# A decoder block's early weight loads, zero fill and convolution taps in another order

## The reference

```python
x = x + attention0(layernorm(x))                    # Fourier features of q and kv, running sum over positions
x = x + conv0(layernorm(x), k, skip, ctx, ctx)      # the sublayer around the change
x = x + experts0(layernorm(x))                      # 8 experts, the best 2 for each row
x = x + attention1(layernorm(x))
x = x + cross_attention1(layernorm(x), ctx)
x = x + ternary_ffn1(layernorm(x))

def conv0(v, k, bias, x1, x2):                      # num_heads = 8, 16 groups, L = 256 channels
    vr, x1r, x2r = (t.reshape(B, 16, 8, L) for t in (v, x1, x2))
    kv = vr[:, :, :, None, :] * x2r[:, :, None, :, :]
    y = causal_convolution(kv, k)                   # by FFT in the reference: y[l] = sum over m <= l of k[l-m] kv[m]
    y = y + kv * skip
    return einsum('bhijl,bhil->bhjl', y, x1r)
```

## Time and profile before

| | |
|---|---|
| median of 3 executions | 808.7 us (807.49, 808.7, 815.94) |
| the profiled execution | 810.86 us |
| its span, first to last instruction | 809.0 us |
| PE, PEld busy | 626.0 us (77%), 440.7 us (54%) |
| DVE busy | 456.6 us (56%) |
| ACT busy | 321.5 us (40%) |
| POOL busy | 261.6 us (32%) |
| DMA | 50.01 MB, 62 GB/s over the span |
| mean granted clock of TensorE | 0.879 |

### The profile page before, as it was taken

The page is one execution under the profiler, slowest core; times in us unless marked ns, Lnnn a source line. Parts: engine busy times, 40 slices in busy tenths (PEclk is TensorE's granted clock), DMA queues, the critical chain, the costliest instruction groups (busy, mean ns, idle before and its releaser), DMA issues.

```text
span 809.0 us, 13184 instructions
## 1 busy us (share of the span) xinstructions
PE 626.0 (77%) x4335; PEld 440.7 (54%) x4338; DVE 456.6 (56%) x988; ACT 321.5 (40%) x754; POOL 261.6 (32%) x300
## 2 busy tenths in 40 slices
PE   3849897450599999997387998999988767774564
PEld 3446444430488988896363456555576346553233
DVE  4684999575355554553225153352547755777685
ACT  2503200424133343342233364553736445555353
POOL 5470588748000000000702882763904220000000
PEclk9969999555799999999558999999999988996697
DMA  9930001456611111111800000000000400000000
GB/s 328 375 123 1 0 0 60 148 164 239 198 50 33 49 52 52 52 40 37 244 8 0 1 1 0 0 0 0 0 1 1 156 1 2 2 2 1 0 26 26
DMA packets 35589, 50.01 MB, mean 62 GB/s; under 512 B 3288, under 2 KB 26400, under 8 KB 35296
## 3 DMA queue, kind: packets, MB, share of 16 engines
q1 hardware_dynamic: 33024, 41.39, 15.7%
q0 software_dynamic: 2528, 8.13, 2.7%
HBM read 38.50 MB, written 11.01 MB: 61 GB/s over the span
## 4 chain that ended last, share of the span: by engine, by line
PE 65%; DVE 14%; ACT 10%; POOL 4%; issue 3%; DMA 3%; another core or an unknown queue 1%; SPq 0%; ACTq 0%; DVEq 0%; POOLq 0%
PE bank L1491 15%; PE bank L1504 5%; PE bank L1608 4%; PE bank L1607 4%; PE bank L1662 4%; POOL sorted_rows L481 3%; PE bank L1629 3%; PE bank L1379 2%; ACT sm L689 2%; PE bank L1423 2%; PE bank L1424 2%; PE bank L1422 2%; PE bank L1362 2%; DVE xn L881 2%; PE bank L1621 2%
## 5 line engine op out<-in xcount | busy, mean ns | idle before, releaser
L644 ACT ACTIVATE hf<-bank,be 128x256 f32<-128x256 f32 x120 | 50.5, 472 | 85.6 <-PE bank L1491 71.8
L1491 PE MATMUL bank<-h,wsp 128*128 128x256 f16 x720 | 81.3, 273 | 2.0 <-DVE h L1059 1.4
L1491 PEld LDWEIGHTS bank<-h,wsp 128*128 x720 | 69.4, 98 | 12.1 <-issue 3.7
L487 POOL DMA_INDIRECT yg<-expert_rows,pos x16 | 15.8, 988 | 185.0 <-DMA expert_rows<-yb 180.5
L1057 DVE CAST h<-hf 128x512 f16<-128x512 f32 x60 | 25.6, 427 | 64.4 <-ACT hf L644 62.8
L559 ACT CAST wsp<-wraw 128x2048 f16<-128x2048 f32 x12 | 22.6, 1900 | 74.4 <-DMA wraw<-in_L_ffn_W 74.4
L1160 DVE SCALAR_TENSOR_TENSOR sm<-bank,const 128x512 f32<-128x512 f32 x32 | 22.1, 691 | 50.2 <-PE bank L1629 50.2
L689 ACT ACTIVATE sm<-sm,nm 128x128 f32<-128x128 f32 x128 | 50.0, 395 | 0.9 <-DVE nm L1163 0.9
L450 POOL TENSOR_TENSOR wsp<-wraw,wsp 128x512 f16<-128x512 f32 x40 | 46.0, 1182 | 8.5 <-ACT wsp L559 8.2
L497 POOL TENSOR_TENSOR rq<-qs,const 128x256 f32<-128x256 f32 x32 | 23.2, 725 | 77.3 <-ACT qs L695 77.2
L469 POOL TENSOR_TENSOR kvp<-xnT,cxT 128x512 f32<-128x512 f32 x32 | 34.8, 1110 | 40.2 <-DVE xnT L886 32.2
(11 more groups left out here) (302 smaller groups left out, 1409.9 us busy)
## 6 DMA issues: line engine op xcount, KB each, us to landing
wraw<-in_L_ffn_W SPq DMA_DIRECT2D x16, 512.0 KB, 4.3
wraw<-in_L_ffn_W SPq DMA_DIRECT2D x8, 1024.0 KB
sorted_rows<-early POOLq DMA_DIRECT2D x2, 1920.0 KB, 15.4
xg<-sorted_rows SPq DMA_DIRECT2D x15, 256.0 KB, 2.8
expert_rows<-yb SPq DMA_DIRECT2D x15, 256.0 KB, 2.2
tapR<-in_kpad SPq DMA_DIRECT2D x16, 128.0 KB, 12.7
x<-in_x SPq DMA_DIRECT2D x1, 1024.0 KB, 5.9
cx<-in_ctx SPq DMA_DIRECT2D x1, 1024.0 KB, 11.7
```

The costliest lines, as they stand in the source:

```text
L644: last = nc.scalar.activation(hf[:, p, SLOTS * k:SLOTS * k + SLOTS], bank[2 * (layer - 1) + p][:, SLOTS * k:SLOTS * k + SLOTS], ACT.Gelu, ...
L1491: last = nc.tensor.matmul(b[:, SLOTS * (f % 2):SLOTS * (f % 2) + SLOTS], w[a_][:, c, P * f:P * f + P], inp[:, b_, c, :], start=(c == 0 and ...
```

## The change

It has four parts. SP issues both halves of experts 0 and 1 ahead of `cx`, and the taps behind `cx` in one load of 2 MB. POOL issues the two zero fills after its four splits, not ahead of them. The host lays out the Toeplitz matrices, `taps`, [128, 16 x 256], so that the reversed loads, the eight matmuls, the eight copies and the constant `reverse` are gone. DVE does `xnT_copies(2)` ahead of the four `wsk`.

```diff
--- before.py
+++ after.py
@@ -35,7 +35,7 @@
 U32 = mybir.dt.uint32
 
 
-EARLY = ("fourier", "inverse", "reverse", "group8")
+EARLY = ("fourier", "inverse", "group8")
 
 
 def shape_constants():
@@ -44,7 +44,6 @@
     parts = {}
     parts["ident"] = np.eye(P)
     parts["upper"] = np.triu(np.ones((P, P)))
-    parts["reverse"] = np.eye(P)[::-1]
     parts["group8"] = np.kron(np.eye(HG), np.ones((CH, CH)))
     parts["ones"] = np.ones((P, P))
 
@@ -175,7 +174,7 @@
         const12 = sb("const12", [P, ncol - nlate], F32, s3e)
         cst.update({name: const12[:, lo - nlate:hi - nlate] for name, (lo, hi) in CONST_AT.items() if name in EARLY})
         s1, s2 = ExitStack(), ExitStack()
-        tapR = sb("tapR", [P, HG, D], F32, s3e)
+        tap = sb("tap", [P, HG, D], F32, s3e)
         skip = sb("skip", [P, 1], F32, s3e)
         wq = sb("wq", [P, DC, D], F32, s1)
         wkv = sb("wkv", [P, DC, D], F32, s1)
@@ -192,7 +191,6 @@
         kqT = sb("kqT", [P, 4, 512], F32, s1)
         pr = sb("pr", [P, 2, 4, P], F32, s1)
         s1.close()
-        tap = sb("tap", [P, HG, D], F32, s2)
         wsk = sb("wsk", [P, NT, D], F32, s2)
         sk2 = sb("sk2", [P, 2, 512], F32, s2)
         kvp = sb("kvp", [P, 2, DC, 512], F32, s2)
@@ -353,13 +351,12 @@
                                  a["L0_ffn_W2"][e].rearrange("(c p) n -> p c n", p=P)).then_inc(sem("w_loaded_odd"), 16)
 
             expert_half(0, 0)
+            expert_half(0, 1)
+            for half in range(2):
+                expert_half(1, half)
             sp.dma_start(cx[:], a["ctx_2048"].rearrange("b s d -> s b d")).then_inc(sem("s2_loaded"), 16)
-            expert_half(0, 1)
-
-            for h in range(HG):
-                pad = a["kpad"]
-                src = bass.AP(tensor=pad.tensor, offset=pad.offset + h * (P + D) + 1, ap=[[1, P], [1, D]])
-                sp.dma_start(tapR[:, h, :], src).then_inc(sem("s2_loaded"), 16)
+
+            sp.dma_start(tap[:].rearrange("p h n -> p (h n)"), a["taps"]).then_inc(sem("s2_loaded"), 16)
             with nc.allow_non_contiguous_dma(reason="one value per partition"):
                 sp.dma_start(skip[:], a["fside_S2_0"].rearrange("(p o) -> p o", o=1)).then_inc(sem("s2_loaded"), 16)
             sp.dma_start(wg[:], a["L0_ffn_Wg"].rearrange("(c p) e -> p c e", p=P)).then_inc(sem("gate_loaded"), 16)
@@ -372,7 +369,7 @@
                 if e == NE // 2:
                     x_done(sp, 2, NT - 1)
                 for half in range(2):
-                    if e:
+                    if e >= 2:
                         expert_half(e, half)
 
             def rows_in(i, u):
@@ -431,11 +428,6 @@
             unused = early[:, NE // 2 - 1].rearrange("p a n -> p (a n)").bitcast(F32)
             zeros = unused[:, 0:ET * D].rearrange("p (b d) -> p b d", d=D)
             nc.gpsimd.memset(unused, 0.0).then_inc(sem("zeroed"), 1)
-            pool.wait_ge(sem("zeroed"), 1)
-            pool.wait_ge(sem("w1_loaded"), 48)
-            for k in range(2):
-                rows = ET * P
-                pool.dma_start(xs[rows * k:rows * k + rows, :].rearrange("(b p) d -> p b d", p=P), zeros).then_inc(sem("zero_filled"), 16)
 
             def split_low(k):
 
@@ -458,6 +450,10 @@
                 last.then_inc(sem("w_hi_pool"), 1)
                 split_low(k)
 
+            pool.wait_ge(sem("zeroed"), 1)
+            for k in range(2):
+                rows = ET * P
+                pool.dma_start(xs[rows * k:rows * k + rows, :].rearrange("(b p) d -> p b d", p=P), zeros).then_inc(sem("zero_filled"), 16)
             pool.wait_ge(sem("xnT_act"), 4)
             pool.wait_ge(sem("xnT_dve"), 4)
             pool.wait_ge(sem("cxT_ready"), 4)
@@ -592,9 +588,6 @@
                     act.wait_ge(sem("products_ready"), t - 3)
                 nc.scalar.copy(kqT[:, t % 4, :], bank[4 + t % 4][:]).then_inc(sem("kqT_ready"), 1)
 
-            for k in range(8):
-                act.wait_ge(sem("tap_psum"), k + 1)
-                nc.scalar.copy(tap[:, 2 * k:2 * k + 2, :].rearrange("p h n -> p (h n)"), bank[4 + k % 2][:]).then_inc(sem("tap_ready"), 1)
             deviation(2)
             for half in range(2):
                 for c in range(DC):
@@ -933,13 +926,13 @@
             add_attention(NT - 1)
 
             layernorm(2)
-            dve.wait_ge(sem("s2_loaded"), 16 * (HG + 2))
+            dve.wait_ge(sem("s2_loaded"), 48)
+            xnT_copies(2)
             for k in range(4):
                 two = slice(2 * k, 2 * k + 2)
                 dve.wait_ge(sem("xn_ready"), NT + 2 * k + 2)
                 nc.vector.scalar_tensor_tensor(wsk[:, two, :], xn[:, two, :], skip[:, 0:1], cx[:, two, :],
                                                ALU.mult, ALU.mult).then_inc(sem("wsk_ready"), 1)
-            xnT_copies(2)
             for k in range(4):
                 two = slice(2 * k, 2 * k + 2)
                 dve.wait_ge(sem("skip_psum"), k + 1)
@@ -1394,12 +1387,7 @@
             attention_out(NT - 1)
 
             pe.wait_ge(sem("kqT_ready"), NT)
-            pe.wait_ge(sem("s2_loaded"), 16 * (HG + 2))
-            for k in range(8):
-                if k >= 2:
-                    pe.wait_ge(sem("tap_ready"), k - 1)
-                nc.tensor.matmul(bank[4 + k % 2][:], cst["reverse"], tapR[:, 2 * k:2 * k + 2, :].rearrange("p h n -> p (h n)"),
-                                 start=True, stop=True).then_inc(sem("tap_psum"), 1)
+            pe.wait_ge(sem("s2_loaded"), 48)
             for half in range(2):
                 for c in range(DC):
                     if half:
@@ -1408,7 +1396,6 @@
                         last = nc.tensor.transpose(bank[6 + c][:, P * k:P * k + P], cx[:, 4 * half + k, P * c:P * c + P], ident)
                     last.then_inc(sem("cxT_psum"), 1)
             transposes(2)
-            pe.wait_ge(sem("tap_ready"), 8)
             pe.wait_ge(sem("cxT_ready"), 4)
             for k in range(4):
                 pe.wait_ge(sem("wsk_ready"), k + 1)
@@ -1935,9 +1922,10 @@
     nc = _bacc.Bacc("TRN2", target_bir_lowering=False, num_devices=1)
     host = {name: np.ascontiguousarray(inputs[name]) for name in _INS}
     taps = inputs["L0_xattn_k"]
-    kpad = np.zeros((taps.shape[0], P + D), np.float32)
-    kpad[:, P:] = taps
-    host["kpad"] = kpad
+    padded = np.zeros((taps.shape[0], P + D), np.float32)
+    padded[:, P:] = taps
+    lag = P + np.arange(D)[None, :] - np.arange(P)[:, None]
+    host["taps"] = np.ascontiguousarray(padded[:, lag].transpose(1, 0, 2).reshape(P, HG * D))
     host["wkvT"] = np.ascontiguousarray(inputs["L1_xattn_wkv"].T)
     host["consts"] = shape_constants()[0]
     arrays, args = {}, {}
```

## The result

The changed kernel takes 805.98 us in the median of 22 runs (797.93 to 811.21), the kernel before 810.4 on the same chip (22 runs, 806.01 to 816.01). The ratio is 0.9927 with a 95% interval of 0.9903 to 0.9952: 5.9 us less, within 1%. The ratio compares the means of the fast runs, which leaves out two of the changed kernel's 22, over 1.5% above its fastest; the two medians as they stand differ by 4.4 us. The forecast was 6.0 us less, 802.7 us with a range of 799.5 to 806.5, so the measured time lies near the range's upper end: the kernel before, 808.7 us in the three runs that the forecast was built on, took 810.4 in the 22. The profiled execution took 805.3 us, with a span of 803.5 (before 809.0) and a mean granted clock of 0.875 (before 0.879).

The account below looks back on a forecast made before the run. The bound was the chain of waits through PE, DVE, ACT and POOL, not DMA. Loads 0.6 plus taps and order 6.0 less clock 0.6 gave 6.0 us: 808.7 to 802.7, range 799.5 to 806.5.

Parts of the forecast that it names:

- Loads: Before attention: POOL splits from 15 to 44, first eight L907 disturbed, last eight free; first `pr` 0.6 us earlier.
- Zero fill: POOL's issue moves to about 44, beside DVE's inverse norms and L907, which lose 0 to 1 us; taken as 0.
- Taps: Before layernorm 2: DVE's 6.22 us wait for the square root falls to 0.3; xn is done 5.95 us earlier.
- Order on DVE: After xn: POOL's products start 8.0 us earlier, `wsk` takes 4.8, convolution starts 5.0 earlier, loop ends 6.0 earlier.
- the clock's fall: Before the convolution loop: TensorE's slower clock lengthens transposes and `group8` matmuls, costing 1.2 us; half, 0.6, is counted.
- Behind the loop: After the convolution loop: nothing changes, so the lead stays the same at the scatters and the experts' first matmul.
- Rival B: `wsk` and POOL's products don't hinder each other and the clock holds; loop ends at 127.4, total 800.0 us; chance 0.15.
- C: Up to the first `pr`: POOL's splits disturb all norms and L907; gain left 2.4 us, total 806.3; chance 0.15.
- D: In the convolution loop: TensorE's clock stays at 1.2 GHz; six such groups lose 15.5 us, total 818; chance 0.08.

Follow-up runs that it names:

- The loads alone: Kernel before with only the early expert loads and the zero fill behind the splits; tap matmuls and DVE order as before: ratio 0.9983.
- The repeated execution: The changed kernel once more, unedited, on the same chip as the last three kernels: 803.95 us against 812.85 for the kernel before, ratio 0.9888.
- the taps alone: Kernel before with only the host-made taps in one load; loads, zero fill and DVE order as before: ratio 0.9945.
- `wsk`-first kernel: Changed kernel with DVE forming the four `wsk` ahead of its `xnT` copies again, as before: ratio 0.9884.
- the four later kernels: `wsk` first, with POOL's splits in 256 columns (0.9896), DVE's remainders also cut (0.9796), mixed pieces (0.9776), expert 1's splits put off, 512 columns (0.9779).
- the last group: On one chip beside the kernel before: changed kernel repeated (0.9888), mixed pieces (0.9776), expert 1's splits put off in 256 (0.9768) and 512 columns (0.9779).

## Why the prediction held, step by step

**Loads.** Right. POOL's splits ran without a gap from 15.00 to 43.5 (forecast 44). The first eight scalings were slow (they lost 4.1 us, forecast 4.2) and the last eight undisturbed. PE had its first `pr` 0.8 us earlier (forecast 0.6); DVE began it at the same instant (49.28, before 49.29), and the 0.8 lie in the `pr`, which now run undisturbed. The loads alone gave 1.5 us at the loop's end. It is a shift of the disturbance, as "GPSIMD Engine Reference", Key points, of the Trainium skill, cited in the prediction, also had it. The runs add the size of the wait: it is what remains of the partner's current instruction.

**Attention tiles.** Not forecast: PE's last attention matmul is 2.2 us earlier, though its start is only 0.8 earlier. In the changed kernel PE's first tiles run at half clock for 3 us, before for 6. The windows of the changed kernel:

```profile
50.20:53.20 3.00, 3.00 (x7) 2.44 (x8) 0.65 (x3) 0.00 (x0) 0.00 (x0) 0.50 1.03 410
53.20:57.20 4.00, 4.00 (x25) 3.62 (x25) 2.52 (x7) 0.99 (x2) 0.00 (x0) 0.98 1.02 400
```

and of the kernel before:

```profile
53.20:57.20 4.00, 4.00 (x14) 3.38 (x13) 2.68 (x6) 0.59 (x1) 2.35 (x3) 0.51 0.02 8
```

PE was busy for all 4.00 us in both, at 0.51 before and 0.98 after. The repeated execution has 0.86 in this window. By the trace's clock, over ten executions of changed kernels with DVE's first `pr` at 49 to 50.4, it came back between 53.3 and 57.2, in the kernel before at 57.1. The two at 57 are the kernel before and the taps alone, in which POOL still split expert 1 until 55.5 and 53.9 and slowed the `pr`; the nine with the early loads have 53.3 to 55.8. So a part of these 1.4 us may belong to the loads and not to chance. What sets the instant is open.

**Zero fill.** Taken at nothing for DVE, within bounds of 0 to 1 us. It cost 0.6. While POOL issued it, from 43.50 to 46.19, DVE's L853 took 0.85 us and ended at 46.23; in the kernel without expert 1's splits, where POOL was idle then, the same instruction took 0.23. The two-input steps beside it (0.29) weren't held. The repeated execution has 0.86. Its other effect was not in the prediction. Behind the splits it leaves the DMA engines to the weights, and ahead of them it costs 4.4 us of POOL's end and 0.9 of the first `pr`.

**Taps.** Right in kind and size. The wait of 6.22 us fell to 0.28, so 5.94 were freed, not the 7.14 of the matmuls. The taps alone gave 5.7 at the loop's end, although their last attention add came 1.6 us later than before (73.80, before 72.17); their loop didn't meet the fall of the clock that the kernel before has at its start.

**Order on DVE.** Each landmark was close: `wsk` took 5.17 us (forecast 4.8). `kvp` began 9.2 us earlier, where 8.0 and the attention tiles' 2.2 would have made it 10.2. The first `yx` was at 89.32, where the forecast's 90.2 on the old scale, or 91.4 with the clock's fall, less those 2.2, are 88.0 and 89.2. The clock did fall where I had put the risk, twice. Of the changed kernel:

```profile
73.00:77.00 4.00, 3.15 (x17) 2.91 (x16) 3.16 (x9) 1.65 (x3) 0.00 (x0) 0.60 0.00 0
80.00:84.00 4.00, 3.71 (x5) 1.39 (x5) 4.00 (x4) 1.33 (x1) 4.00 (x3) 0.58 0.00 0
```

What failed here is not a term but a question that wasn't asked. The sum priced the new order against the kernel before, where it came with the taps' removal, and never against the change without it. By the `wsk`-first kernel this part costs 3.1 us. The first fall of the clock isn't the reason: the four later kernels with `wsk` first at 53.0 us had one too, between 71 and 79. The second, from 80.6 to 84.0, stands only in the four executions in which `wsk` runs beside POOL's products, and what it adds is in the 3.1. What was needed stood in the sum already: `wsk` at 4.8 instead of 2.65, on the chain, for products that weren't on it.

**Behind the loop.** "Unchanged" held up to the experts (6.5, 6.9, 7.1). Then 1.4 us went by the granted clock in the 642 to 731 stretch, which no part of the change touches.

So the agreement, 5.9 against 6.0, is partly luck. In the profiled execution two errors stand against each other: some 1.4 us more in the attention tiles, 1.4 less in the later stage, both by when the clock was granted. And the same kernel repeated in the last group gained 8.9. Rival B, `wsk` undisturbed, is refuted by 5.17 against 2.73. C is refuted by the last eight scalings at 2.77; its sum was also off, as 8 x 0.4 and 8 x 0.9 make 10.4 and not 10, which leaves a gain of 2.0 us and 806.7. D didn't occur, since from 90.74 on PE ran the loop's pairs at 1.10 us and less.

## What to carry to other kernels

Before moving a helper engine's work, look at what its partner does at the new place. Under attention tiles, where DVE mostly waits for PE, POOL's splits of expert 1 moved the last tile by 1.2 us (256 columns) or 2.6 (512), against the kernel that leaves them out (last add at 64.08); under two-input instructions on the chain they cost 5.8. Where the two must overlap, cut the pieces of both so that a wait is short, but only there, since each cut costs the helper overhead. Price every reordering against the same change without it, not only against the kernel before.

## What the runs showed of the hardware

- A DVE instruction with two inputs in SBUF is held until POOL's current copy, subtraction or product ends, and so is a `TENSOR_SCALAR` with one, as layernorm's scaling of xn. Eight columns took 0.17 us alone, 0.53 and 1.08 us beside pieces of 256 and 512. Adds from PSUM (0.41), reductions (0.69) and reciprocals (0.94) were not held.
- It holds in the other direction too: a scatter's issue on POOL went from 0.96 to 2.99 us beside DVE's 2048-column subtraction, and to 1.4 beside one of 512.
- Beside POOL's issue of the zero fill only the one-input kind was held: two-input steps took their 0.29 us, the `TENSOR_SCALAR` 0.85 us instead of 0.23.
- Halving POOL's pieces from 512 to 256 columns made half an expert's split 7.9 us instead of 6.8, without any contention.
- One stage of nearly the same kernels took 236 to 238 us on one chip and 250 to 251 on others, while the stage ahead of it agreed within 1.5 us (176.9 to 178.4 from `xg` to `wkvb`).
